# Graph network on one core: GpSimd makes the own loop's share of two attention outputs, and VectorE joins the ELU in one operation

## What is computed

```python
x = layernorm(x + L0(x, edges, edge_attr))     # edge MLP, mean, node MLP
x = layernorm(x + L1(x, edges))                # two attention convolutions
x = layernorm(x + L2(x, edges))                # three SAGE convolutions
x = layernorm(x + L3(x, edges, edge_attr))     # softmax aggregation
```

```python
def gat_conv(x, src, dst, W, att_src, att_dst, bias, heads, out_c):
    h = (x @ W).reshape(n, heads, out_c)
    e = leaky_relu(a_src[src] + a_dst[dst], 0.2)
    p = exp(e - segment_max(e, dst)[dst])
    alpha = p / (segment_sum(p, dst)[dst] + 1e-16)
    return segment_sum(h[src] * alpha, dst) + bias
h   = elu(gat_conv(x, src + loop, dst + loop, W1, ..., b1, 4 heads))
out = gat_conv(h, src + loop, dst + loop, W2, ..., b2, 1 head)
```

## Time and profile before

| | |
|---|---|
| Median of 3 runs | 4085.72 us (4085.16 to 4087.35) |
| Span of the profiled execution | 4084.8 us |
| Busy: PE, DVE, ACT, POOL | 2340.4, 2167.9, 1837.8, 2646.4 us |
| Share of the chain that ended last: POOL, issue, PE, DVE | 51%, 19%, 12%, 11% |

### The profile page before, as it was taken

How to read it: one execution, slowest core, us unless ns; L and a number is a source line. 1 busy time by engine, 2 the same in 40 slices (tenths; PEclk the granted TensorE clock), 3 DMA queues, 4 the chain that set the end, 5 groups by cost and what they waited for, 6 DMA issues and landing times.

```text
span 4084.8 us, 45091 instructions
## 1 busy us (share of the span) xinstructions
PE 2340.4 (57%) x10010; PEld 1833.9 (45%) x10010; DVE 2167.9 (53%) x5164; ACT 1837.8 (45%) x4303; POOL 2646.4 (65%) x2793
## 2 busy tenths in 40 slices
PE   6777785344442444444555566655755555477776
PEld 5665653334342434442333354443544344365554
DVE  6888873556565555554222233333434444666668
ACT  3887874334332434335343344334253432444443
POOL 4777712777753777744777727777467776577771
PEclk8999997555556555555555577778855555788886
DMA  6555512333322334324655523333267777455551
GB/s 194 158 161 155 161 54 52 81 84 82 82 58 59 81 77 84 77 48 112 159 158 158 158 85 105 106 105 105 64 187 209 213 212 199 125 155 155 156 159 41
DMA packets 589398, 497.69 MB, mean 122 GB/s; under 512 B 73851, under 2 KB 530608, under 8 KB 588800
## 3 DMA queue, kind: packets, MB, share of 16 engines
q0 software_dynamic: 101696, 235.14, 23.1%
q1 hardware_dynamic: 484630, 254.57, 22.5%
q10 hardware_dynamic: 2828, 5.18, 0.4%
HBM read 426.04 MB, written 68.57 MB: 121 GB/s over the span
## 4 chain that ended last, share of the span: by engine, by line
POOL 51%; issue 19%; PE 12%; DVE 11%; DMA 4%; DVEq 1%; ACT 1%; POOLq 0%; SPq 0%; ACTq 0%
POOL big L597 24%; POOL big L610 18%; POOL y_and_h L624 9%; PE ps L744 5%; DVE y_and_h L1395 3%; DMA big<-table_sage,src_block 2%; DVE ps L1387 2%; PE ps L666 2%; DVE big L1367 2%; PE ps L895 1%; PE ps L680 1%; PE ps L892 1%; DVEq L418 1%; DVEq L1387 1%; DVE x_sb L1500 1%
## 5 line engine op out<-in xcount | busy, mean ns | idle before, releaser
L597 POOL DMA_INDIRECT big<-table_sage,src_block x1173 | 1109.5, 946 | 550.3 <-issue 347.2
L610 POOL DMA_INDIRECT big<-table_gat,src_idx x832 | 787.1, 946 | 479.6 <-issue 247.5
L1367 DVE TENSOR_TENSOR big<-big,ps 128x257 f32 (+3 forms) x1664 | 591.8, 356 | 219.1 <-issue 15.9
L624 POOL DMA_INDIRECT y_and_h<-table_pool,src_block x391 | 377.7, 966 | 166.7 <-issue 118.9
L597 POOL DMA_INDIRECT big<-table_mlp,src_block x391 | 371.3, 950 | 159.8 <-issue 117.4
L1154 ACT ACTIVATE rows<-iota,dst_rel 128x128 f32<-128x128 f32 x768 | 243.7, 388 | 260.2 <-PE ps L895 172.3
L1367 DVE TENSOR_TENSOR y_and_h<-y_and_h,ps 128x256 f32 x416 | 175.0, 421 | 338.9 <-PE ps L892 293.4
L1176 ACT ACTIVATE y_and_h<-y_and_h 128x128 f32<-128x128 f32 (+1 forms) x26 | 8.0, 309 | 677.0 <-DVE y_and_h L1607 677.0
L744 PE MATMUL ps<-w_sb,ea_sb 128*128 128x256 f32 x832 | 213.0, 400 | 126.8 <-DVE y_and_h L1395 115.6
L1798 DVE TENSOR_TENSOR_SCAN big<-ps,big 128x512 f32<-128x512 f32 x98 | 125.4, 1280 | 282.5 <-PE ps L921 279.6
L1849 DVE TENSOR_TENSOR_SCAN ps<-ps,small,big 128x512 f32<-128x512 f32 (+1 forms) x98 | 126.3, 1289 | 252.9 <-PE ps L921 209.0
(11 more groups left out here) (302 smaller groups left out, 5643.8 us busy)
## 6 DMA issues: line engine op xcount, KB each, us to landing
big<-in_ea_blocks SPq DMA_DIRECT2D x194, 256.0 KB, 4.1
ea_sb<-in_ea_blocks SPq DMA_DIRECT2D x416, 64.0 KB
ea_sb<-rel_rows SPq DMA_DIRECT2D x208, 128.0 KB
prefix_blocks<-big SPq DMA_DIRECT2D x97, 256.0 KB, 2.5
big<-prefix_blocks SPq DMA_DIRECT2D x97, 256.0 KB, 4.1
below_blocks<-big SPq DMA_DIRECT2D x97, 256.0 KB, 2.7
rows<-in_ea_rows SPq DMA_DIRECT2D x97, 256.0 KB
big<-table_sage,src_block POOLq DMA_INDIRECT x1173, 2.8
```

The source lines that it names most:

```text
L597: pool.indirect_dma_start(ring[:, (block + RING_FIRST[k]) % (n * G), :], None, table[k], bass.IndirectOffsetOnAxis(src_block[:, block:bloc ...
L610: pool.indirect_dma_start(ring[:, step % GAT_RING, :], None, table[k], bass.IndirectOffsetOnAxis(src_idx[:, step:step + 1], 0))\
L624: pool.indirect_dma_start(pool_rows[q][:, i, :], None, table["pool"], bass.IndirectOffsetOnAxis(src_block[:, block:block + 1], 0)).then_in ...
L1367: dve.tensor_tensor(to, to, bank_of(j), ALU.add).then_inc(accumulated, 1)
```

## The change

POOL gets a new function, `weigh_loops`, between its gathers: pack by pack it multiplies the own rows by their share (L639 of the changed kernel) and adds the bias of `gat1`, or the residual for `gat2` (L644). DVE keeps the edge sums (L1727) and one addition (L1732) for `gat1`, and one fused operation per tile for `gat2` (L1717); it works out the own loop's share ahead of the edges' factor. For the ELU, DVE takes maximum and sum in one operation (L1741), ACT's scratch becomes `xT`, and the minus one goes into ACT's copy of the turned rows, as a bias.

```diff
+            def weigh_loops(k):
+                n, heads = GAT[k]
+                pool.wait_ge(shares_ready, n + 1)
...
+                for u, tiles in enumerate(packs(4)):
...
+                    pool.tensor_tensor(loop[:, at, :].rearrange("p t (f h) -> p t f h", h=heads),
+                                       h_sb[:, at, 0:D].rearrange("p t (f h) -> p t f h", h=heads), over, ALU.mult)\
+                        .then_inc(loops_weighed, 1)
+                    other = x_sb[:, at, :] if heads == 1 else spread("gb1").unsqueeze(1).to_broadcast([P, len(tiles), D])
+                    pool.wait_ge(loops_weighed, n * NPACK + u + 1)
+                    pool.tensor_tensor(loop[:, at, :], loop[:, at, :], other, ALU.add).then_inc(loops_made, 1)
             gather_steps("gat1")
+            weigh_loops("gat1")
             gather_steps("gat2")
+            weigh_loops("gat2")
...
+                        ins = act.activation(to[:, at], bank, ACT.Identity, bias=less)
...
-            copy_turned("gT", big[:, 3, :])
+            copy_turned("gT", big[:, 3, :], neg_one[:, 0:1])
...
+                dve.tensor_tensor(sm(4), sm(4), sm(0), ALU.mult).then_inc(shares_ready, 1)
                 link(dve.tensor_tensor(sm(3), sm(3), sm(0), ALU.mult))
-                link(dve.tensor_tensor(sm(4), sm(4), sm(0), ALU.mult))
...
+                    def add_edges_to_rest(u):
+                        dve.wait_ge(loops_made, first + u + 1)
                         for t in packs(4)[u]:
...
+                            ins = dve.scalar_tensor_tensor(y_sb[:, t, :], acc[:, t, 0:D], small[:, 3, t:t + 1], loop[:, t, :],
                                                            ALU.mult, ALU.add)
...
                 def add_loop(u):
                     dve.wait_ge(edges_weighed, first + u + 1)
-                    dve.wait_ge(loops_weighed, first + u + 1)
+                    dve.wait_ge(loops_made, first + u + 1)
...
+                dve.scalar_tensor_tensor(y_sb[:, of_pack(u), :], y_sb[:, of_pack(u), :], 0.0,
+                                         low_side.rearrange("p (t f) -> p t f", t=NT)[:, of_pack(u), :],
+                                         ALU.max, ALU.add).then_inc(g1_ready, 1)
...
-            in_packs(*attention_output("gat1", attention_pass("gat1"), "gb1"), pause, pause, positive_side, join_elu)
+            in_packs(*attention_output("gat1", attention_pass("gat1")), pause, pause, join_elu)
```

More of the change, by code:

```diff
@@ L626, in gather_rows_of_pool @@
                             bass.IndirectOffsetOnAxis(src_block[:, block:block + 1], 0)).then_inc(pool_gathered[q], 16)
+            def weigh_loops(k):
+                n, heads = GAT[k]
+                pool.wait_ge(shares_ready, n + 1)
+                share = small[:, 4, 0:NT * heads].rearrange("p (t h) -> p t h", t=NT)
+                loop = spare.rearrange("p (t f) -> p t f", t=NT)
+                for u, tiles in enumerate(packs(4)):
+                    at = slice(tiles[0], tiles[-1] + 1)
+                    over = share[:, at, :].unsqueeze(2).to_broadcast([P, len(tiles), D // heads, heads])
+                    pool.tensor_tensor(loop[:, at, :].rearrange("p t (f h) -> p t f h", h=heads),
[4 more added lines that the diff above has]
+                    pool.tensor_tensor(loop[:, at, :], loop[:, at, :], other, ALU.add).then_inc(loops_made, 1)
             pool.wait_ge(src_loaded, 16)
@@ L1055, in copy_rows, with copy_turned @@
                     act.activation(to[:, tiles[0]:tiles[-1] + 1, 0:width], bank, func).then_inc(read_by["act"], 1)
[L1057 removed]
+            def copy_turned(name, to, less=None):
                 for u, tiles in enumerate(packs(4)):
[L1059 to L1061 removed]
+                    at, bank = slice(tiles[0] * P, (tiles[-1] + 1) * P), filled(name, u)[:, 0:len(tiles) * P]
+                    if less is None:
+                        ins = act.activation(to[:, at], bank, ACT.Copy)
+                    else:
+                        ins = act.activation(to[:, at], bank, ACT.Identity, bias=less)
+                    ins.then_inc(read_by["act"], 1)
             low = big[:, 0:2, :].rearrange("p a n -> p (a n)").rearrange("p (t f) -> p t f", t=NT)
@@ L1683, in attention_output @@
                 link(dve.reciprocal(sm(0), sm(0)))
+                dve.tensor_tensor(sm(4), sm(4), sm(0), ALU.mult).then_inc(shares_ready, 1)
                 link(dve.tensor_tensor(sm(3), sm(3), sm(0), ALU.mult))
-                link(dve.tensor_tensor(sm(4), sm(4), sm(0), ALU.mult))
+                loop = spare.rearrange("p (t f) -> p t f", t=NT)
+                first = n * NPACK
                 if heads == 1:
-                    def add_edges_to_residual(u):
+                    def add_edges_to_rest(u):
+                        dve.wait_ge(loops_made, first + u + 1)
                         for t in packs(4)[u]:
[L1690 to L1697, removed]
+                            ins = dve.scalar_tensor_tensor(y_sb[:, t, :], acc[:, t, 0:D], small[:, 3, t:t + 1], loop[:, t, :],
                                                            ALU.mult, ALU.add)
                         ins.then_inc(y_made, 1)
-                    return add_edges_to_residual, add_own_loop
-                loop = spare.rearrange("p (t f) -> p t f", t=NT)
-                first = n * NPACK
-                def over(a, u):
-                    return a[:, of_pack(u), :].unsqueeze(2).to_broadcast([P, len(packs(4)[u]), D // heads, heads])
+                    return add_edges_to_rest,
                 def heads_of(a, u):
@@ L1710, in weigh_edges @@
                 def weigh_edges(u):
[L1711 to L1716, removed]
+                    over = sm(3)[:, of_pack(u), :].unsqueeze(2).to_broadcast([P, len(packs(4)[u]), D // heads, heads])
@@ L1724, in add_bias @@
[L1724 to L1727, removed]
                        .then_inc(attended, 1)
-                return weigh_edges, weigh_loop, add_loop, add_bias
+                return weigh_edges, add_loop
             dve.wait_ge(read_by["act"], fills_read(FIRST_FILL["gT"], "act"))
```

17 lines of the change are left out of this document (6 added, 11 removed).

## The result

The changed kernel takes 4096.27 us (median of 11 runs, 4093.21 to 4099.34), the kernel before in the same rounds 4086.54 (11 runs, 4082.28 to 4087.8). The ratio is 1.0024, with an interval of 1.0015 to 1.0033: slower by 9.7 us, where 9.3 was forecast. The profiled execution has a span of 4096.8 us, 12.0 more than before; it took 4098.59 us, 2.3 above its median.

The account below looks back on a forecast made before the run. The prediction took DVE to pace both outputs, with POOL idle there. Turns would lose 6.0 us in the first and 3.3 in the second: 4085.7 + 9.3 = 4095.0 us, range 4077 to 4104.

Parts of the forecast that it names:

- POOL's 13P: Each output: POOL's 13 whole-pack operations in series, each of length P, 15.6 us.
- tail: What follows POOL's last operation: 4.4 us to the first output's product, 3.7 to the second's variance.
- turns: POOL and two-SBUF-input DVE operations exclude each other, adding 10.2 and 6.4 us; either form, P 0.98 to 1.41: chance 0.63.
- P: Length of one POOL operation on a whole pack of 512 numbers: taken as 1.20 us, ends 0.55 and 1.41.
- The case of no waiting: Both outputs: POOL and DVE work side by side unhindered, gaining 4.2 and 3.1 us, 7.3 in all; chance 0.24.
- the last rival: Second output: one fused tile passes per POOL operation, 7.4 us lost, kernel 4099.1; chance within the 0.63 for turns.
- the main case: Turns at P of 1.20: 6.0 us lost in the first output, 3.3 in the second, kernel 4095.0; likeliest case.
- 15.6 + 10.2 + 4.4: First output: POOL's time, turns and tail put the product 30.2 us after the share against 24.2, 6.0 lost.
- 3.4 + 4.2 + 3.7 - 0.52: Second output, the last rival: remaining 13 tiles, row sums and squares, and tail without its 0.52, behind POOL's end at 19.0.
- What was counted as nothing: ACT's part, including the bias in its copies, lies beside POOL; the last copy costs 0.1 us of the path.
- six of the seven lie beside the transposes: First output's end: six of ACT's seven copies are covered by transposes, 4 x 0.26 us for a pack.

Follow-up runs that it names:

- experiment 1: The changed kernel with a PSUM bank (ones, not the computation's values) as second operand of DVE's operations in both outputs: 4080.14 us in one run.
- experiment 3: The changed kernel, but DVE begins its packs of an output only when POOL has made all seven shares: 4104.96 us in one run.
- 2: The changed kernel with each pair of POOL operations replaced by one memset, so that POOL only writes: 4074.53 us in one run.
- 9: The changed kernel with ACT's copies of turned packs placed four packs behind their ELU operations instead of all at the end: 4096.4 us in one run.
- 6: The kernel before with POOL's share in the second output (gat2) alone, first output as before: 4086.96 us against 4082.68, ratio 1.001.
- 5: The kernel before with only the ELU part of the change, POOL having no part: 4082.47 us against 4082.68, ratio 1.0.
- 7: The changed kernel with ACT's plain copy of the turned packs, without the minus one as bias: 4091.68 us in one run.
- experiment 4: The changed kernel, same computation, with operands through PSUM so DVE reads at most one tensor from SBUF: 4081.16 us against 4085.74 before, ratio 0.9992.
- 8: The kernel before with the ELU part, and ACT instead of POOL multiplying own rows by their share for gat2: 4081.03 us against 4082.68, ratio 0.9998.

## Why the prediction was right

Counted as the prediction counts, from the end of the share's multiplication, with POOL's own time and the tail behind it taken from experiment 1 and the turns as the difference to the changed kernel:

| | POOL's 13P | tail | turns | sum | before |
|---|---|---|---|---|---|
| first output, forecast | 15.6 | 4.4 | 10.2 | 30.2 | 24.2 |
| first output, measured | 15.6 | 5.8 | 6.9 | 28.3 | 24.3 |
| second output, forecast | 15.6 | 3.7 | 6.4 | 25.7 | 22.4 |
| second output, measured | 15.6 | 5.2 | 6.2 | 27.0 | 22.4 |

**POOL's price** was right. A pair of operations takes 2.34 us (1246.51 to 1248.85 in experiment 3), 1.17 each; the half pack, at 0.61 and 0.72 by the same profile, costs more than half, so that the fourteen come to 15.6 (1240.11 to 1255.71 in experiment 1). That P was put at 1.20 and the half pack at half hits the sum by a little luck: 13 x 1.17 is 15.2.

**That they take turns in both directions** was right, and is shown: with one operand in PSUM both engines run at their own lengths (1), and POOL writing alone leaves DVE's at 0.68 (2), though there the overlap is short (3.11 us in each output). The forecast's turns of 10.2 and 6.4 assume that a POOL operation holds DVE too, which no row of before shows. The changed kernel shows it: the edge sums at 1249.52, begun 0.39 us into POOL's L644 of 1249.13, took 1.75 us for 0.68 before. The case of no waiting, to which the prediction gave 0.24, has by its terms 4078.4 at P = 1.20, and 4072.7 to 4083.9 over a P of 0.98 to 1.41. It fell for the changed kernel; the 4080.14 of experiment 1, where the waiting was taken away, lies in that range.

**How they take turns** was the last rival's: singly. In the second output 11 of 26 tiles had begun when POOL ended, where that rival had 13 done and the main case 24. But POOL was not kept waiting for these tiles as the rival had it: it ended 15.76 us after the share, not 19.0. DVE then needed 11.24, where the rival's terms (3.4 + 4.2 + 3.7 - 0.52) give 10.8. Its 29.8 is 2.8 too high, since POOL did not wait; the main case's 25.7 is 1.3 too low, since more than half the tiles came only behind POOL.

**The step that was mis-sized** is the sum "15.6 + 10.2 + 4.4" of the first output. POOL's operations waited 0.45 and 0.33 us for a DVE operation (1.50 against 1.05, 1.59 against 1.26), not 0.60, and for 12 operations, not 16.5, since no more than one passes for each of POOL's: POOL ended 20.1 after the share instead of 25.8. Eight DVE operations came behind it (1262.73 to 1267.3), where the forecast had the half addition and three joins, and the tail was 8.2 instead of 4.4. It also left out that the last packs' ELU goes through ACT once more (0.42 and 0.83 in the chain) ahead of the copies, and where it has the transposes and one copy on the path (2.6 + 0.53), the chain has all seven copies (3.84).

**What was counted as nothing**, the bias, of which the forecast saw 0.1 on the path, was 0.4 us: "six of the seven lie beside the transposes" does not hold, as all seven copies stand behind ACT's last exponential in its order, and the bias lengthens each. Together with the order of the copies (0.7 us by 9) ACT had a part in the tail that the sum did not have.

**The total** came out at 9.7 against 9.3 by luck: 2.0 us too much in the first output and 1.3 too little in the second nearly cancel, and 8.6 is what the two profiles show in the two outputs. The other 1.1 us are not settled: they are less than one kernel's executions differ by. Whether the product's later rise to full clock in the changed kernel (0.50 from 1270.44, 8.65 us long) belongs to the change stays open too. The two profiles of before have 6.07, the twelve of the other kernels 7.5 to 8.9, but one of these (6) has the first output of before, and it is as long without POOL's pace (5) and without the bias (7).

The division of work itself would have gained a little: without the turns the product came at 22.92 and the variance at 20.79 (4, which also changes DVE's order a little), 3.4 us in all ahead of the kernel before by the two profiles. The interval of the whole time, 0.9983 to 1.0001, just reaches no change.

## What to carry to other kernels

Before work goes from DVE to an idle GpSimd, count how many of DVE's remaining operations there read two tensors from SBUF: here each of them was traded one for one against a GpSimd operation that reads (12 for 12 in the first output), so that of many short ones most came last of all (15 of 26 fused tiles had not begun when POOL ended). Where one operand lay in PSUM the two ran side by side (1, 4: in the first output DVE's pack operations took 0.68 to 0.70, POOL's 1.04 to 1.05 and 1.26 to 1.27), and in the second output ACT took the same share with DVE's operations at 1.13 to 1.14 for four tiles and 0.68 to 0.69 for the addition (8). A tail is traced through every engine's program order, since what is queued there behind a late operation has no cover: ACT, busy 11.46 of 28.26 us in the changed kernel's first output, had its seven copies, 3.84 us, on the path at the end.

## What the runs showed of the hardware

- The turns go one for one: in the changed kernel's first output POOL's last 12 operations (1244.89 to 1261.20) alternate with 12 DVE operations that have two inputs in SBUF (1245.03 to 1261.60), and each of these lasted 1.10 to 1.75 us for 0.68 of its own.
- POOL lost little to short operations: fused tiles of 128x128 lengthened its operations from 1.04 to at most 1.09 us and 1.26 to 1.27, while a tile itself took up to 1.42 instead of 0.34.
- An operation with a single small input was held too. In experiment 4 the scaling of 128x4 numbers beside POOL and, later, without it:

```profile
1844.90 1.05 DVE L1516 TENSOR_SCALAR stat<-stat 128x4 f32<-128x4 f32 x1
...
1855.11 0.15 DVE L1516 TENSOR_SCALAR stat<-stat 128x4 f32<-128x4 f32 x1
```

  Sums over 128x512 (a reduction) were not: in the same run one took 0.67 beside POOL (L1521 at 1852.34, inside POOL's L644 of 1851.68 to 1852.94), and one 0.67 without it (1857.10).
